# First cross-attention: keys of two batches per tile loaded turned, those of the other two turned on TensorE; X in four loads; tile 0 ahead of quarter 1

## The reference

```python
x = x + _L0_xattn_ref(_layernorm(x, axis=-1), ctx_1024, ctx_1024, W1, b1, W2, b2, gamma, beta)
# per batch: softmax(q @ keys.T / sqrt(D)) @ values, keys = values = context rows,
# plus q, a layer norm, relu(z @ W1 + b1) @ W2 + b2 + z, and a second layer norm
```

## Time and profile before

| | |
|---|---|
| median of 3 timed runs | 2211.74 us (2205.1 to 2214.41) |
| span of the profiled execution | 2208.0 us, 3.7 us under that median |
| first layer, to the fence | 0 to 104.7 us |
| granted TensorE clock, mean over the span | 0.913 |

### The profile page before, as it was taken

How to read it: one execution, slowest core, us unless ns; L and a number is a source line. 1 busy time by engine, 2 the same in 40 slices (tenths; PEclk the granted TensorE clock), 3 DMA queues, 4 the chain that set the end, 5 groups by cost and what they waited for, 6 DMA issues and landing times. The chain is left out here.

```text
span 2208.0 us, 49959 instructions
## 1 busy us (share of the span) xinstructions
PE 1833.8 (83%) x20130; PEld 1190.9 (54%) x20130; DVE 1512.9 (69%) x3632; ACT 976.1 (44%) x2471; POOL 729.9 (33%) x951
## 2 busy tenths in 40 slices
PE   6768999899878789986677699999999987757596
PEld 2313556555545556643557466666666652225386
DVE  4799995688875665557861577666766569987732
ACT  3455754566643722242412355555555421115243
POOL 1333554455540524214340501000000046633443
PEclk9878999999999999998779999999999998876698
DMA  9100000100016100070034101000000000021087
GB/s 352 61 1 1 1 1 1 73 4 5 5 77 260 55 2 1 3 322 2 2 118 145 45 20 39 11 20 20 20 11 10 1 1 10 19 91 77 30 289 239
DMA packets 56085, 134.78 MB, mean 61 GB/s; under 512 B 13913, under 2 KB 34092, under 8 KB 48176
## 3 DMA queue, kind: packets, MB, share of 16 engines
q1 hardware_dynamic: 52560, 125.48, 15.9%
q0 software_dynamic: 3296, 6.12, 0.8%
HBM read 112.13 MB, written 20.12 MB: 60 GB/s over the span
## 5 line engine op out<-in xcount | busy, mean ns | idle before, releaser
L317 POOL TENSOR_TENSOR arena<-arena 128x4 f32<-128x4 f32 (+2 forms) x97 | 113.9, 1175 | 816.1 <-DVE arena L261 358.9
L3223 ACT ACTIVATE arena<-PS,arena 128x289 f32<-128x289 f32 x256 | 127.0, 506 | 177.3 <-DVE arena L3328 177.2
L1803 POOL TENSOR_TENSOR arena<-arena 128x128 f32<-128x128 f32 x384 | 140.8, 405 | 44.3 <-PE PS L1666 20.8
L3111 PE MATMUL PS<-arena 128*128 128x289 f32 x512 | 136.2, 409 | 2.3 <-DVE arena L3322 1.8
L1739 DVE RECIPROCAL arena<-PS 128x128 f32<-128x128 f32 x96 | 91.6, 955 | 51.4 <-PE PS L1704 51.2
L1770 ACT COPY arena<-PS 32x128 f32<-32x128 f32 x384 | 99.5, 259 | 51.3 <-PE PS L1680 46.7
L364 PE MATMUL PS<-arena 128*128 128x512 f32 x208 | 110.7, 657 | 12.5 <-DVEq L4134 11.7
L1189 POOL TENSOR_TENSOR arena<-arena 128x512 f32<-128x512 f32 x64 | 84.0, 1313 | 109.6 <-DVE arena L1334 109.6
L3111 PEld LDWEIGHTS PS<-arena 128*128 128x128 f32 x512 | 92.8, 192 | 24.5 <-issue 2.6
L3328 DVE TENSOR_REDUCE arena<-PS 128x2 f32<-128x578 f32 x128 | 92.5, 753 | 7.3 <-PE PS L3111 6.1
L2448 PE MATMUL PS<-arena 128*128 128x512 f32 x192 | 90.9, 608 | 0.0
(11 more groups left out here) (412 smaller groups left out, 4746.0 us busy)
## 6 DMA issues: line engine op xcount, KB each, us to landing
arena<-in_ctx SPq DMA_DIRECT2D x48, 1090.0 KB, 8.9
arena<-in_f_w SPq DMA_DIRECT2D x39, 514.0 KB, 5.6
lists<-arena SPq DMA_DIRECT2D x8, 1040.0 KB, 9.9
arena<-in_f_w SPq DMA_DIRECT2D x32, 256.0 KB, 2.9
arena<-in_ctx SPq DMA_DIRECT2D x16, 512.0 KB, 3.7
arena<-in_mid SPq DMA_DIRECT2D x1, 3796.5 KB, 11.7
arena<-in_late SPq DMA_DIRECT2D x1, 3204.0 KB, 10.3
arena<-in_w SPq DMA_DIRECT2D x1, 3017.0 KB, 13.1
```

The costliest lines, as they stand in the source:

```text
L317: e.tensor_tensor(x, x, half.broadcast_to(list(x.shape)), ALU.pow).then_inc(*T.done("norm_root", tag))
L1803: k = e.tensor_tensor(dst[:, b], spread(src[:, b, :], [P, HG, S], 1), spread(self.g.C["headmask"], [P, HG, S], 2), ALU.mult)
L3111: m = e.matmul(PS[:, k, 0:UL], self.qt[i % 2][:, j, P * k:P * k + P], self.kt[i % 3][:, j, :], start=True, stop=True)
L3223: e.activation(self.weights(n, k, 0, UL), PS[:, k, 0:UL], ACT.Exp, bias=self.st[:, h, k:k + 1], accum_out=self.st[:, h, 4 + k:5 + k]).then ...
```

## The change

The layout of the context in memory becomes: two turned key sets, the turned 257th keys of the other two batches (2 words), the values, the repeated 257th row, and last the other two turned key sets; 2182 words in all. The first layer loads only the first 1668 words. The two missing key sets of 256 rows are made on PE from the values by four transposes (`key_turn`) into PSUM bank 5, copied out by ACT (tiles 0 to 2 and the even ones) or DVE (odd ones from 3 on). `scores` of those two batches waits for that copy, and takes a 256-column and a 1-column matmul each. The fourth and seventh layer load all 2182 words, the tenth has new offsets.

```diff
 class CrossAttention:
-    KEYS, ROWS, LAST = BT * U, BT * 2 * D, D
+    HALF = BT // 2
+    ROWS_AT = HALF * U + HALF
+    LAST_AT = ROWS_AT + BT * 2 * D
+    REST_AT = LAST_AT + D
+    WORDS = REST_AT + HALF * U
+    TURN_BANK, AHEAD = 5, 3
...
+    def keys_turned(self, i):
+        return ("x_kT_dve" if i % 2 and i >= self.AHEAD else "x_kT_act"), (self.tag, i)
...
-            e.dma_start(self.words[i % self.NS], self.g.t["ctx"][i])...
+            e.dma_start(self.words[i % self.NS], self.g.t["ctx"][i][:, 0:self.width])...
...
-            for j in range(BT):
+            for j in range(self.HALF if self.turned else BT):
                 k = e.matmul(PS[S * j:S * j + S, b, 0:U], self.qT[...], self.keys(i, j), start=True, stop=True)
+            if self.turned:
+                for w in T.due(self.keys_turned(i)):
+                    e.wait_ge(*w)
+                for j in range(self.HALF, BT):
+                    q = self.qT[:, P * i + S * j:P * i + S * j + S]
+                    e.matmul(PS[S * j:S * j + S, b, 0:UA], q, self.turned_keys(i, j), start=True, stop=True)
+                    k = e.matmul(PS[S * j:S * j + S, b, UA:U], q, self.lone_key(i, j), start=True, stop=True)
+        def key_turn(i):
+            b = self.TURN_BANK
+            for w in T.due(free[b], self.context(i)):
+                e.wait_ge(*w)
+            for j in range(2 * self.HALF):
+                k = e.transpose(PS[:, b, P * j:P * j + P], self.rows(i, 2 * self.HALF + j), g.C["ident"])
+            k.then_inc(*T.done("x_key_turn", (tag, i)))
+            free[b] = self.keys_turned(i)
...
+        if self.turned:
+            for i in range(self.AHEAD):
+                key_turn(i)
         scores(0)
         scores(1)
+        if first is not None:
+            first()
         for i in range(steps):
             if i + 2 < NT:
                 scores(i + 2)
+            if self.turned and i + self.AHEAD < NT:
+                key_turn(i + self.AHEAD)
             if i < NT:
                 turn(i)
...
     def act(...):
+        def keys_out(i):
+            for w in T.due(("x_key_turn", (tag, i)), ("x_scores", (tag, i - 3))):
+                e.wait_ge(*w)
+            e.copy(self.kT[i % 3], PS[:, self.TURN_BANK, :]).then_inc(*T.done("x_kT_act", (tag, i)))
+        if self.turned:
+            for i in range(self.AHEAD):
+                keys_out(i)
+        if first is not None:
+            first()
         exps(0)
         for i in range(steps):
             if i + 1 < NT:
                 exps(i + 1)
+            if self.turned and i + self.AHEAD < NT and (i + self.AHEAD) % 2 == 0:
+                keys_out(i + self.AHEAD)
...
     def dve(...):
             if i + 1 < NT:
                 maxima(i + 1)
+            if self.turned and i + self.AHEAD < NT and (i + self.AHEAD) % 2:
+                keys_out(i + self.AHEAD)
...
 class L0Cross(Layer):
-        self.x = CrossAttention(g, 0, room, g.XT, ..., self.O, 8, unread=1)
+        self.x = CrossAttention(g, 0, room, g.XT, ..., self.O, NT, turned=True)
...
-        e.dma_start(g.X, t["x"]...).then_inc(*T.done("in_x", 0, 16))
-        e.dma_start(g.const_words, t["const"]).then_inc(*T.done("in_const", 0, 16))
+        for q in range(NQ):
+            e.dma_start(quarter(g.X, q), t["x"][cut(q), :]...).then_inc(*T.done(f"in_x{q}", 0, 16))
+            if q == 0:
+                e.dma_start(g.const_words, t["const"]).then_inc(*T.done("in_const", 0, 16))
...
     def pe(self, e, T):
-        for w in T.due(("in_const", 0), ("in_x", 0)):
+        for w in T.due(("in_const", 0)):
             e.wait_ge(*w)
-        cols_pe(e, T, g, 0, g.XN, free, range(4))
+        def turn(quarters):
+            for q in quarters:
+                cols_pe(e, T, g, 0, g.XN, free, self.COLS, qs=(q,))
+                free[self.COLS[q]] = ("cols_act", (0, q))
+        turn((0,))
...
     def act(self, e, T):
-        cols_act(e, T, g, 0, g.XT, range(4))
+        cols_act(e, T, g, 0, g.XT, self.COLS, qs=(0,))
...
-        self.x.act(e, T, more, self.STEPS)
+        self.x.act(e, T, more, self.STEPS, lambda: cols_act(e, T, g, 0, g.XT, self.COLS, qs=range(1, NQ)))
...
     def dve(self, e, T):
-        for w in T.due(("in_const", 0), ("in_x", 0)):
-            e.wait_ge(*w)
-        norm_dve(e, T, 0, g.XN, g.X, 1e-5, g.small)
-        cols_dve(e, T, g, 0, g.XT, range(4))
+        norm_dve(e, T, 0, g.XN, g.X, 1e-5, g.small, lambda q: [(f"in_x{q}", 0)])
```

More of the change, by code:

```diff
@@ L73 @@
 KIND.update({f"tile{k}": f"context{k}" for k in range(8)})
+KIND.update({"key_turn": "turned", "kT_act": "cols_act", "kT_dve": "cols_dve", "early": "last_in", "x0": "x", "x1": "rows0", "x2": "rows1", "x3": "rows2"})
+KIND.update({f"context{k + 8}": name for k, name in enumerate(("v30", "v31", "v32", "v33", "back0", "back1", "back2", "back3"))})
 def work_of(name):
@@ L611, with __init__ @@
 class CrossAttention:
-    KEYS, ROWS, LAST = BT * U, BT * 2 * D, D
-    def __init__(self, g, tag, room, qT, scale, O, slots, shift=None, unread=0):
+    HALF = BT // 2
[4 more added lines that the diff above has]
+    TURN_BANK, AHEAD = 5, 3
+    def __init__(self, g, tag, room, qT, scale, O, slots, shift=None, unread=0, turned=False):
         self.g, self.tag, self.qT, self.scale, self.O, self.shift, self.NS = g, tag, qT, scale, O, shift, slots
-        self.unread = unread
-        self.words = [room.take(self.KEYS + self.ROWS + self.LAST) for _ in range(slots)]
+        self.unread, self.turned = unread, turned
+        self.width = self.REST_AT if turned else self.WORDS
+        self.words = [room.take(self.width) for _ in range(slots)]
+        self.kT = [room.take(self.HALF * UA) for _ in range(3 if turned else 0)]
         self.pr = [room.take(U) for _ in range(3)]
@@ L651, in sp, with pe @@
                 e.wait_ge(*w)
-            e.dma_start(self.words[i % self.NS], self.g.t["ctx"][i]).then_inc(*T.done(*self.context(i), 16))
-    def pe(self, e, T, free, ready, more, steps, idle):
+            e.dma_start(self.words[i % self.NS], self.g.t["ctx"][i][:, 0:self.width]).then_inc(*T.done(*self.context(i), 16))
+    def pe(self, e, T, free, ready, more, steps, idle, first=None):
         g, tag, PS = self.g, self.tag, self.g.PS
@@ L702, in pe, with act @@
             more(i)
-    def act(self, e, T, more, steps):
+    def act(self, e, T, more, steps, first=None):
         g, tag, PS = self.g, self.tag, self.g.PS
@@ L758, in output, with keys_out @@
                                    op0=ALU.mult, op1=ALU.add).then_inc(*T.done("x_read", (tag, i)))
+        def keys_out(i):
+            for w in T.due(("x_key_turn", (tag, i)), ("x_scores", (tag, i - 3))):
+                e.wait_ge(*w)
+            e.tensor_copy(self.kT[i % 3], PS[:, self.TURN_BANK, :]).then_inc(*T.done("x_kT_dve", (tag, i)))
         maxima(0)
@@ L905, in more @@
                     e.wait_ge(*w)
[L906 removed]
+                e.tensor_tensor(m, four(g.PS[:, 4, :]), m, ALU.add).then_inc(*T.done("rows_read", ("x0_f", q)))
                 norm_stats_dve(e, T, "x0_p", q, tmp, 1e-6, self.small2, lambda q: [("rows_read", ("x0_f", q))], by_act=True)
@@ L4164, in sync_program @@
         e.wait_ge(*w)
-    for w in T.due(*(("out", q) for q in range(NQ)), ("in_x", 0), ("in_const", 0), ("in_weights", "first"), ("in_weights", "mid"), ("in_weights", "late"),
+    for w in T.due(*(("out", q) for q in range(NQ)), *((f"in_x{q}", 0) for q in range(NQ)), ("in_const", 0), ("in_weights", "first"), ("in_weights", "mid"), ("in_weights", "late"),
                    ("f2_slots_in", "zero"), ("f2_slots_in", "rows"), *((f"f2_gathered{q}", 4 * q + 3) for q in range(NQ)), ("f2_scattered", NT - 1),
@@ L4306 @@
     rows = ctx[:, 0:UA].reshape(NT, BT, 2, P, D)
+    keys = ctx.reshape(NT, BT, U, D).transpose(0, 3, 1, 2)
     arrays = {
```

49 lines of the change are left out of this document (28 added, 21 removed).

## The result

The changed kernel takes 2197.9 us (median of 9 runs, 2193.2 to 2201.7), the one before 2210.4 us (9 runs, 2204.8 to 2215.5). The ratio is 0.9946, interval 0.9932 to 0.9960: a gain of 9 to 15 us. Forecast were 2206.2 and a range from 2199.0, so it lies past the fast end of the range. Faster by more than 11 us had been given a chance of 0.15.

What follows compares the result with a forecast made beforehand. The prediction took PE to bound the loop, 1.05 of 2.58 us being an unread filler, with chains at the start and quarter ends. Terms -2.5 - 1.8 + 0.4 - 1.15 + 0.4 - 0.85 = -5.5 gave 2206.2 us, range 2199.0 to 2214.0.

Steps and rivals of the forecast that it cites:

- start, to sums(0): First layer's start: X in four loads and tile 0 ahead of quarter 1 bring sums(0) to 25.6 from 28.06, -2.5 us.
- loop, sums(0) to sums(4): First layer's loop: filler out, four transposes and one-column matmuls in, iteration 2.12 instead of 2.58 us; -1.8 us.
- chain of quarter 0: Residual and norm of quarter 0: a DVE key copy ahead of output(5) delays them, +0.4 us (0 to +1.3).
- to sums(8): From quarter 0 turned: two fillers go, two key turns and two pairs of one-column matmuls come, -1.15 us.
- chain of quarter 1: Residual and norm of quarter 1: DVE is busy there and gets one more key copy, +0.4 us (0 to +0.9).
- to sums(12): After quarter 1: two fillers go, one key turn and the one-column matmuls come, -0.85 us.
- rest of the layer: After iteration 12: no key turns, and quarters 2 and 3 wait for norms left alone; 0, within 1 us either way.
- the full clock back at about 23: Start, main case: PE's full clock returns at about 23 us, as before, so sums(0) is at 25.6, -2.5 us.
- back at 20: Start, alternative case: PE's full clock returns at 20 us, making the start's gain -4.5 us.
- Rival A: Start: clock returns while quarters are turned, X lands early, whole head start kept; -9 to -12, about 2201.5 us; chance 0.17.
- Rival B: Loop: key copies 0.4 us late each iteration pace it at 2.5 us; near -1, 2210.5 us; chance 0.13.
- Rival C: Loop: PE falls to the half clock without fillers, iteration 3.3 us; about +5, 2217 us; chance 0.10.

Runs made afterwards that it cites:

- a_again: The changed kernel, unchanged, run again for a second profile: 2198.23 us (one run).
- b_nofill: The kernel before without the 512-column fillers ahead of the scores, context blocks still whole: 2197.28 us, ratio to before 0.9927.
- a_look3: The changed kernel, unchanged, run for a third profile: 2197.28 us (one run).
- b_x4_nofill: The kernel before with X in four loads and without fillers, whole context blocks in eight buffers: 2199.82 us, ratio 0.9951.
- a_full8: The changed kernel with whole context blocks of all key sets in eight buffers and no key turns: 2200.14 us, ratio 0.9945.
- a_nokeys: The changed kernel's small blocks without key turns, their copies and one-column matmuls, leaving out half of the scores' keys; not a usable version: ratio 0.9937.
- b_x4: The kernel before with X in four loads, constants second, fillers kept: 2207.03 us, ratio 0.9982.
- a_fill: The changed kernel with one 512-column filler put back ahead of each scores: 2210.17 us, ratio 0.9987.

## Why the forecast fell short

Terms as forecast, against the first pair of profiles and against the means of five profiles of the changed kernel and two of the kernel before (us):

| term | forecast | first pair | means |
|---|---|---|---|
| start, to sums(0) | -2.5 | -5.3 | -4.7 |
| loop, sums(0) to sums(4) | -1.8 | -2.2 | -2.2 |
| chain of quarter 0 | +0.4 | +0.3 | +0.3 |
| to sums(8) | -1.15 | -2.3 | -1.4 |
| chain of quarter 1 | +0.4 | +0.2 | +0.2 |
| to sums(12) | -0.85 | -2.7 | -1.8 |
| rest of the layer | 0 | -0.1 | -0.6 |
| sum | -5.5 | -12.0 | -10.2 |

Terms are rounded. The mean, -10.2, is inside the interval of the timed runs, -15 to -9.

**The step that failed is the start**, and in it the time at which the clock comes back. The path was right to the third key turn and ran 0.5 to 0.8 early: the norm applied at 7.98 (forecast 8.5), quarter 0 turned at 9.24 (9.7), the third key turn at 14.62 (15.4), scores(0) at 15.67 (16.4). What failed came next: "quarters 1 to 3 are turned from 18.5 to 21.5" and "the full clock back at about 23". They were turned from 17.72 to 19.33, almost all at the full rate, and the exponential came 2.3 us sooner than said. I tied the return of the clock to "as much work before 23", by position in time. In all five profiles it came while these quarters were turned: the twelve transposes take 1.61 us in the first, 1.86 in a_again and 2.50 to 2.69 in the other three, where 3.0 were forecast, and the scores behind them (19.33 to 20.18) have the full rate. By then PE had gone without a wait from the third key turn through eight scores into the quarters. Of the 2.5 us by which sums(0) beat the forecast of 25.6 in the mean, 1.1 are the earlier landings, up to the quarters' start, 0.8 the twelve transposes, and 0.6 the two iterations behind them (3.45 against 4.1); the last two, 1.4 together, come with the clock. What was forecast with the clock "back at 20" was -4.5, against a measured mean of -4.7: the case that was priced and not taken.

The forecast's words for this stretch also miss work. It says that PE needs "scores(2), a key turn and turn(0) until sums(0), and no two fillers of 1.5 to 1.9 us". But sums(0) stands in iteration 1, so scores(3), a key turn and turn(1) come first too, and before the change four fillers stood ahead of it, the first two at 19.38 and 22.24 and these:

```profile
24.27 1.13 PE L364 MATMUL PS<-arena 128*128 128x512 f32 x2
...
26.17 1.02 PE L364 MATMUL PS<-arena 128*128 128x512 f32 x2
```

To the next start they take 1.85, 1.46, 1.05 and 0.95 us, 5.3 in all. b_nofill bears that out: with X and the order of the turns as they were, scores(0) starts at 19.33 instead of 21.23, one filler sooner, and sums(0) 4.7 sooner. That is as much as the whole change gains at the start.

**The second error is a size**, behind the quarters. Both terms kept the half clock for part of the stretch, as in the one profile I had. Three of five executions have it (-0.8 and -1.1, close to the forecast), two don't (-2.3 and -2.7). A term whose price depends on that needed an average, -1.4 and -1.8. In the first pair these two terms miss by 3.0 us together, more than the start's 2.8; that the first profile had no fall is luck.

**The loop** was forecast at 2.12 and measured at 2.03 on average (8.13 for four): the sums took 0.46 to the next start instead of 0.59, when matmuls of another shape followed. The one-column matmuls cost 0.15 from 29.96 to 30.11, as bounded from the rows. The Trainium skill, "TensorE: Matmul & The Clock Gate", section "Back-to-back issue gap", would have made them 0.25 without hardware decode; the trace has 0.04 per record and doesn't bear it out here. "The loop is bound by PE" was true with the fillers and hid the limit behind it: without them the old blocks are bound by the queue, and the change brings PE and queue to within 0.03 us of each other (2.04 and 2.01).

**Rival A** comes nearest: the clock came back while the quarters were turned, and the time is past its 2201.5. Its mark, the first exponential before 20, was just missed, at 20.00 and in the other four profiles at 20.00 to 20.77. **Rival B** is out: no wait for key copies paces the loop. Only two waits of 1.6 us in all are theirs, and both are in the quarters' chains, which came out at +0.3 and +0.2 where +0.4 was forecast for each. **Rival C** is out for this kernel: in the loop, 28 to 32, the granted clock is 1.00 in the first profile and in a_look3, with six transposes per iteration. The same page of the Trainium skill, "Part 4: PE-mode transpose", says that transposes don't count as PE busy in the way that matmuls do. This loop spends 0.80 of 2.04 us on them and holds 2.4 GHz, but the other 1.24 us are matmuls, so it doesn't decide whether transposes count; it shows that this share of them brought no fall.

**No version beats the change clearly.** b_nofill, which removes one argument, measures the same; b_x4_nofill and a_full8 do too. a_nokeys ends the layer 3.6 to 6.6 us before the changed kernel's five profiles, which says roughly, from one profile, what cheaper key turns could still bring; no such kernel was built, and in the timed runs even a_nokeys isn't told from the change (the intervals overlap).

## What to carry to other kernels

Before costing a large edit, run its smallest piece alone: a filler that is taken out along the way can bring as much as the whole edit. Price a filler by what it takes at the half rate at the start and ask what the engine would wait for without it; here it hid a queue as slow as the loop with it, 2.66 us per block against 2.58, and the parts of the change that relieve the queue paid only for the work they added. Take several profiles of the same kernel before pricing a fall of the clock: here the first two of the changed kernel agreed, and the next three did not.

## What was not expected of the hardware

Identical programs get the clock differently: no fall until past 60 us in two of five profiles, falls to 1.2 GHz at about 39 to 41 and 56 in the other three, worth 2.5 us of this layer. At the start the granted clock reads 1.00 in the stretches while four transposes take 0.97 to 1.05 us, against 0.49 later (30.11 to 30.60); the durations, not the clock's column, tell the rate there. And fillers of 512 columns, with PE kept busy all of 28 to 32, did not keep the clock up over the quarter's wait: it fell behind quarter 0 in both profiles of the kernel before and in b_x4, as in three of five of the changed kernel, which has none. In a_fill, which has them too, it did not fall there.
